# Gated attention with a routed mixture of experts: slot tiles loaded in pairs, positions made one step sooner, zeros on ScalarE's queue, late low parts on GpSimd

## The reference

```python
xn = layernorm(x)
q, k, v = split(xn @ w_qkv.T + b_qkv)
s = (softmax(q @ k.T / sqrt(512)) @ v) @ w_out.T + b_out          # attention, one head of width 512
vals, idx = top_k(xn @ router_w + router_b, 2)                    # 8 experts, 2 per token
h = silu(xn @ expert_w[e] + expert_b[e])                          # for the chosen experts e
y = xn + (sum of h, weighted by softmax(vals)) @ proj_w + proj_b
out = x + s * silu(norm_w * y / rms(y))
```

## Time and profile before

| what | value |
|---|---|
| median of 3 runs | 536.72 us (535.99 to 538.28) |
| profiled execution, its own time | 537.63 us |
| span of its trace | 535.7 us |
| TensorE busy | 499.5 us, 93% |
| VectorE busy | 305.9 us, 57% |
| ScalarE busy | 204.1 us, 38% |
| GpSimd busy | 178.7 us, 33% |

### The profile page before, as it was taken

How to read it: one execution, slowest core, us unless ns; L and a number is a source line. 1 busy time by engine, 2 the same in 40 slices (tenths; PEclk the granted TensorE clock), 3 DMA queues, 4 the chain that set the end, 5 groups by cost and what they waited for, 6 DMA issues and landing times.

```text
span 535.7 us, 7525 instructions
## 1 busy us (share of the span) xinstructions
PE 499.5 (93%) x2234; PEld 411.1 (77%) x2235; DVE 305.9 (57%) x462; ACT 204.1 (38%) x300; POOL 178.7 (33%) x278
## 2 busy tenths in 40 slices
PE   4999999999999949578989999999999999999996
PEld 2688778887898837466767888789888889888884
DVE  2557232764224315499768888875565753667552
ACT  0264542143023133345333444432364553335550
POOL 3053210003888730000000000157457754275144
PEclk9999999999999969879999999999999999999999
DMA  7761269992786777585767555698513632252202
GB/s 268 263 237 39 95 218 400 406 408 103 229 281 237 255 256 215 158 230 165 211 214 218 190 193 179 205 351 297 192 64 118 197 102 76 71 154 91 79 21 98
DMA packets 69836, 104.22 MB, mean 195 GB/s; under 512 B 7200, under 2 KB 31280, under 8 KB 69808
## 3 DMA queue, kind: packets, MB, share of 16 engines
q1 hardware_dynamic: 60576, 75.26, 41.9%
q0 software_dynamic: 7360, 25.19, 13.7%
q10 hardware_dynamic: 1872, 3.41, 2.1%
HBM read 60.32 MB, written 43.52 MB: 194 GB/s over the span
## 4 chain that ended last, share of the span: by engine, by line
PE 55%; SPq 13%; POOL 10%; issue 8%; DMA 6%; DVE 6%; ACT 1%; DVEq 0%; ACTq 0%; POOLq 0%
PE ab L1394 10%; PE ab L1395 10%; PE ab L1396 10%; SPq L459 9%; POOL rows_scratch L652 6%; PE sc L1394 5%; PE sc L1396 5%; PE sc L1395 5%; PE tp L1400 3%; PE sc L1411 3%; POOL W L641 3%; SPq L502 2%; DMA y_scratch<-yt 2%; DVE tp L1175 2%; PE tp L1445 2%
## 5 line engine op out<-in xcount | busy, mean ns | idle before, releaser
L663 POOL DMA_INDIRECT y<-y_scratch,pos x32 | 31.3, 980 | 159.7 <-DMA y_scratch<-yt 144.4
L1394 PE MATMUL ab<-W,st_h 128*128 x156 | 63.9, 410 | 14.8 <-DVE st_l L1122 9.9
L1395 PE MATMUL ab<-W,st_h 128*128 x156 | 62.5, 400 | 0.0
L1396 PE MATMUL ab<-W,st_l 128*128 x156 | 62.4, 400 | 0.0
L652 POOL DMA_INDIRECT rows_scratch<-xb,pos x32 | 31.2, 974 | 63.7 <-DVEq L1118 55.5
L1394 PEld LDWEIGHTS ab<-W,st_h 128*128 128x128 f32 x156 | 30.4, 195 | 26.1 <-issue 20.0
L1394 PE MATMUL sc<-xt_h,t_h 128*128 128x512 f32 x128 | 50.3, 393 | 0.0
L1396 PE MATMUL sc<-xt_h,t_l 128*128 128x512 f32 x128 | 49.9, 390 | 0.0
L1395 PE MATMUL sc<-xt_l,t_h 128*128 128x512 f32 x128 | 49.8, 389 | 0.0
L868 ACT ACTIVATE yt<-yt 128x512 f32<-128x512 f32 x39 | 24.6, 632 | 48.9 <-DVE yt L1252 48.9
L1183 DVE TENSOR_REDUCE small<-sc 128x1 f32<-128x1024 f32 x16 | 19.6, 1224 | 31.8 <-PE sc L1396 31.7
(11 more groups left out here) (257 smaller groups left out, 1230.2 us busy)
## 6 DMA issues: line engine op xcount, KB each, us to landing
rows_scratch<-xn SPq DMA_DIRECT2D x3, 3328.0 KB, 24.4
y_scratch<-yt SPq DMA_DIRECT2D x39, 256.0 KB, 2.2
xb<-in_expert_w POOLq DMA_DIRECT2D x6, 1024.0 KB, 6.1
xn<-rows_scratch SPq DMA_DIRECT2D x96, 64.0 KB, 2.0
xg<-rows_scratch SPq DMA_DIRECT2D x92, 64.0 KB, 2.2
rows_scratch<-xs SPq DMA_DIRECT2D x16, 256.0 KB, 2.0
xb<-rows_scratch SPq DMA_DIRECT2D x16, 256.0 KB, 7.3
x<-in_x SPq DMA_DIRECT2D x16, 256.0 KB, 2.8
```

What stands on the lines that cost most here:

```text
L663: pool.indirect_dma_start(y[:, q, :], None, y_d, bass.IndirectOffsetOnAxis(pos[:, GB * s + p:GB * s + p + 1], 0))\
L1394: nc.tensor.matmul(dst, lh, rh, start=start, stop=False)
L1395: nc.tensor.matmul(dst, lh, rl, start=False, stop=False)
L1396: return nc.tensor.matmul(dst, ll, rh, start=False, stop=stop)
```

## The change

Six edits: (a) the last piece of `choose` runs after `pt_low(1)` and before `attn_out(0)`; `early_high(0)` moves from query tile (0, 2) to (0, 1), GpSimd makes `early_low(2, ...)` in scatter tiles 12 to 15 in place of 8 to 11, and the loads of rows to send are regrouped. (b) The zero DMAs leave by ScalarE's queue, during the values of batch 0. (c) Slot tiles are loaded two at a time, with four DMAs of 128 KB and two semaphores. (d) The first loads are reordered in SP's queue, and the two peeled `w_low` with `turn` and `g_low` in VectorE's. (e) The low parts m = 2 to 9 are GpSimd's (`w_lp`), m = 0 and 1 stay VectorE's (`BY_VEC = 2`). (f) `mw` is written in another order of columns, so that `key_weights` reads whole blocks.

```diff
-        EARLY_AT = ((0, 2), (0, 3), (1, 0), (1, 3))
+        EARLY_AT = ((0, 1), (0, 3), (1, 0), (1, 3))
+        BY_VEC = 2
+        def lows_done(k):
+            m = 2 * (k + 1 - EARLY)
+            return (w_lo, m) if m <= BY_VEC else (w_lp, m - BY_VEC)
@@ SyncE
-            def load_tile(i, q):
+            def load_pair(i, n, tiles=2):
                 for a in range(4):
-                    sp.dma_start(rows[q][32 * a:32 * (a + 1), :].rearrange("p (r f) -> p r f", r=4),
-                                 rows_q[ds(i, 1), a, :, :, :].rearrange("o s r f -> s (o r) f")).then_inc(xg_in[q], 16)
-            def load_next(i, q):
-                sp.wait_ge(g_t, i - 3)
-                load_tile(i, q)
+                    w = slice(32 * a, 32 * (a + 1))
+                    sp.dma_start(pairs[n][w, 0:tiles, :].rearrange("p t (r f) -> p (t r) f", r=4),
+                                 rows_q[ds(i, tiles), a, :, :, :].rearrange("t s r f -> s (t r) f"))\
+                        .then_inc(pair_in[n], 16)
+            def load_next(i, n, tiles=2):
+                sp.wait_ge(g_t, i - 2)
+                load_pair(i, n, tiles)
-            sp.wait_ge(zero_set, 1)
-            for n in range(3):
-                w = slice(n * SLOT_TILES // 3, (n + 1) * SLOT_TILES // 3)
-                sp.dma_start(rows_t[:, w, :], zeros.to_broadcast([P, w.stop - w.start, D])).then_inc(zero_in, 16)
             for j in range(GB):
                 (bias loads at j == QB + 1 as before)
+                if j == QB + 2:
+                    sp.wait_ge(ptr_done, 1 + GB)
+                    load_pair(2, 1)
+                if j == QB + 3:
+                    load_next(6, 1)
                 sp.wait_ge(ab_read, 2 + U["a", 0, j] + 1)
                 sp.dma_start(s_g[j], so[:, j % 2, :]).then_inc(so_st[j % 2], 16)
                 if 1 <= j <= 3:
-                    for g in range(GB + 2 * j - 2, GB + 2 * j if j < 3 else G):
+                    for g in range(GB + 3 * j - 3, min(GB + 3 * j, G)):
                         load_to_send(g)
-                if j == QB + 1:
+                if j == QB:
                     for g in range(GB):
                         sp.wait_ge(sent[g], 64)
-                    for i in range(2):
-                        load_tile(i, i)
+                    load_pair(0, 0)
                 if j == QB + 2:
-                    (loads of tiles 2 and 3, then 4 to 7 behind the loop)
+                    load_next(4, 0)
@@ the looped tiles
-                for q in range(4):
-                    store_y(4 * i + q, q % 2)
-                    load_next(4 * i + q + 8, q)
+                for n in range(2):
+                    store_pair(4 * i + 2 * n)
+                    load_next(4 * i + 2 * n + 8, n)
@@ GpSimd
-                if g < 3 * KC:
+                if g < 2 * KC:
                     early_low(g // KC, g % KC)
+                elif g >= 3 * KC:
+                    early_low(2, g % KC)
             for c in range(KC):
                 early_low(3, c)
+            for m in range(BY_VEC, LATE):
+                _, whole, high, low = halves(m)
+                pool.wait_ge(w_hi, m + 1)
+                pool.tensor_tensor(low, whole, high, ALU.subtract).then_inc(w_lp, 1)
@@ ScalarE
+            def clear_slots(n):
+                w = slice(n * SLOT_TILES // 3, (n + 1) * SLOT_TILES // 3)
+                act.dma_start(rows_t[:, w, :], zeros.to_broadcast([P, w.stop - w.start, D])).then_inc(zero_in, 16)
                 v_hi(0, t)
+                if t >= GB - 3:
+                    act.wait_ge(zero_set, 1)
+                    clear_slots(t - GB + 3)
             def load_next(k):
-                act.wait_ge(w_lo, 2 * (k - 1 - EARLY))
+                act.wait_ge(*lows_done(k - 2))
@@ VectorE
                 pt_low(1)
+                go_on()
                 attn_out(0)
                 row_max(QB * i + 3)
-                go_on()
...
             for i in range(PEEL):
                 add_bias(i, i % 2, i < 2)
                 g_low(i + 2, i % 2)
                 turn(i + 4, i % 4, i // 4 + 1)
-                if i < LATE - AHEAD:
-                    w_low(i + AHEAD)
@@ fold of the keys (n >= KC), high and low parts alike
+                    out, whole = by_fours(out), in_fours(whole)
@@ TensorE, key_weights
-                    last = product(bank(("t", b, i, n)), every_fourth(left[:, 0, c, :], n), every_fourth(left[:, 1, c, :], n),
+                    w = slice(n * P, (n + 1) * P)
+                    last = product(bank(("t", b, i, n)), left[:, 0, c, w], left[:, 1, c, w],
                                    right[0][:, c, q], right[1][:, c, q], c == 0, c == KC - 1)
```

More of the change, by code:

```diff
@@ L216, in gated_attention_moe @@
         rows = (xn[:, 0, :], xn[:, 1, :], xg[:, 0, :], xg[:, 1, :])
+        pairs = (xn, xg)
         mw1_rows = mw1[:, :, :, :].rearrange("p a c n -> p (a c) n").bitcast(F32)
@@ L298, in gated_attention_moe @@
         w_lo = sem("w_lo")
+        w_lp = sem("w_lp")
         be_in = sem("be_in")
-        xg_in = sems("xg_in", 4)
+        pair_in = sems("pair_in", 2)
         g_t = sem("g_t")
@@ L350, in home, with in_fours, by_fours @@
             return SLOT_TILES + (g + GB if g < GB else g - GB)
+        def in_fours(v):
+            return v.rearrange("p (q c) -> p q c", c=KC)
+        def by_fours(v):
+            return v.rearrange("p (c q) -> p q c", c=KC)
         def raw_in(k):
@@ L746, in fold_high @@
                 k = n if n < KC else FOLDS[n - KC]
-                nc.scalar.copy((nw_h if n < KC else mw_h)[:, k, :], sc[:, k // 2, k % 2, :]).then_inc(fold_h, 1)
+                out, whole = (nw_h if n < KC else mw_h)[:, k, :], sc[:, k // 2, k % 2, :]
+                if n >= KC:
+                    out, whole = by_fours(out), in_fours(whole)
+                nc.scalar.copy(out, whole).then_inc(fold_h, 1)
             def normalise(g):
@@ L875, in load_next @@
             def load_next(k):
-                act.wait_ge(w_lo, 2 * (k - 1 - EARLY))
+                act.wait_ge(*lows_done(k - 2))
                 load_raw(act, k)
             act.wait_ge(s_done, GB)
-            for m in range(AHEAD):
-                w_high(m)
-                if m == 1:
-                    load_next(BY_POOL)
-                    g_split(0, 0, True)
-                    g_split(1, 1, True)
+            w_high(0)
+            w_high(1)
+            g_split(0, 0, True)
+            g_split(1, 1, True)
+            load_next(BY_POOL)
+            w_high(2)
+            w_high(3)
             for i in range(PEEL):
@@ L1024, in fold_low @@
                 k = n if n < KC else FOLDS[n - KC]
-                vec.tensor_tensor(l[:, k, :], sc[:, k // 2, k % 2, :], h[:, k, :], ALU.subtract).then_inc(fold_l, 1)
+                low, whole, high = l[:, k, :], sc[:, k // 2, k % 2, :], h[:, k, :]
+                if n >= KC:
+                    low, whole, high = by_fours(low), in_fours(whole), by_fours(high)
+                vec.tensor_tensor(low, whole, high, ALU.subtract).then_inc(fold_l, 1)
             def fold_value_bias():
@@ L1170, in turn @@
             def turn(i, q, j, first=False):
-                dve.wait_ge(xg_in[q], 64 * (j + 1))
+                dve.wait_ge(pair_in[q // 2], 64 * (j + 1))
                 if not first:
@@ L1230, in attention_block @@
                     turn(1, 1, 0, True)
-                    w_low(0)
-                    w_low(1)
-                attn_out(2)
-                if tail:
-                    g_low(0, 0)
-                    turn(2, 2, 0)
-                    g_low(1, 1)
-                    turn(3, 3, 0)
-                    w_low(2)
-                    w_low(3)
+                    for m in range(BY_VEC):
+                        w_low(m)
+                    g_low(0, 0)
+                    g_low(1, 1)
+                    turn(2, 2, 0)
+                    turn(3, 3, 0)
+                attn_out(2)
                 attn_out(3)
@@ L1672, in attend_late @@
                 attend(1, j, high, low, v1_h, v1_l)
-            pe.wait_ge(w_lo, LATE)
+            pe.wait_ge(w_lp, LATE - BY_VEC)
             turn_comb(0)
```

39 lines of the change are left out of this document (19 added, 20 removed).

## The result

The changed kernel takes 512.04 us (median of 4 runs, 506.97 to 512.65) against 537.50 (535.99 to 538.88) for the kernel before beside it: a ratio of 0.951 (95% interval 0.944 to 0.957). On a second chip six runs gave 515.35 (510.05 to 517.67) against 537.51, a ratio of 0.960 (0.958 to 0.963). The profiled execution took 512.65, its span is 510.8. Forecast were 507 for the median and 507.7 for the profiled execution. The time lies in the stated range of 502 to 516, but 1 us above the likeliest branch (502 to 511), and 5.0 us of the forecast gain of 29.9 are missing. Single executions on the second chip reached 517.67, above the range.

What follows compares the result with a forecast made beforehand. TensorE, busy 93%, was taken as the bound, losing 33.2 us between 189.8 and 341.29; 29.7 + 0.7 - 0.5 = 29.9 us off 537.63 gave 507.7 profiled, 507 median, range 502 to 516.

Steps and rivals of the forecast that it cites:

- (a) Positions: Routing and scatter: `routed` 9.3 us sooner, scatter landed at 182.1, gaining 7.2 us of TensorE idle and half clock behind it.
- R4: Rival at the scatter: it comes no sooner, as zeros or a raw set hold GpSimd; 517 us, chance 0.05.
- (b) Zeros: Zero DMAs on ScalarE's queue: third issue held until 57.5 to 59.5, price 0.5 us; otherwise they cost the scatter 4 us.
- R1: Rival in batch 0's values: early zeros hold up ScalarE or the row stores, 2 to 7 us, about 513; chance 0.15.
- (c) The loop: Looped slot tiles: SP's issues per pair take 4.5 us against TensorE's 5.46, so TensorE sets the pace, 2.73 a tile.
- R3: Rival in the looped tiles: they miss 2.73 us, half of the loop's 8 us stays; 511 us, chance 0.10.
- The peel: First slot tiles: bank free and tile 0 at 200.3, stalls of 1.4, 0.8, 1.1 us, tile 7 ends at 226.1.
- R5: Rival: slower, as a pair of slot tiles lands late; gain gone at a landing of 8.6 us; chance 0.02.
- the prediction's three causes: Lost TensorE time: scatter wait 7.23 us, VectorE's 3.55 us peel step against 2.73, SP's load issuing in looped tiles.
- R2: Rival in the peel: its weight chain is longer than stepped, 3 to 6 us and a half-clock spell; 512, chance 0.13.
- (e): Peel: VectorE's step without `w_low` falls from 3.55 to 2.35 us, under TensorE's 2.73.
- (f): `key_weights`: matmuls 0.2276 us apart instead of 0.2347, 192 of them save 1.4 us; strided folds up to as much again.

Runs made afterwards that it cites:

- f_positions_late: attn_first with the last piece of the routing (`choose`) moved back behind `row_max(3)`: 523.66 us, 0.973.
- f_zeros_on_sp: attn_first with the three zero DMAs back on SyncE's queue, behind the first eight `load_to_send`: 518.98 us, 0.964.
- f_single_loads: attn_first with each pair of slot tiles loaded by eight DMAs of 64 KB instead of four of 128 KB: 527.95 us, 0.983.
- attn_first: Changed kernel with VectorE's `attn_out(2)` and `attn_out(3)` put before the turns of tiles 2 and 3: 510.66 us, 0.949.
- store_first: attn_first with the load of tiles 6 and 7 issued behind the last store of the attention output: 509.82 us, 0.947.
- changed_again: The changed kernel unedited, run again on the second chip: 515.35 us, 0.960.
- f_lows_on_vector: attn_first with the low parts m = 2 to 9 back on VectorE: 511.31 us, 0.951.

## Why the prediction came out as it did

**(a) Positions: the times right, the use of them other than forecast.** GpSimd's first and last issue of the scatter, then ScalarE's copy for expert 1 and the exponential behind it:

```profile
119.20 1.08 POOL L669 DMA_INDIRECT rows_scratch<-xb,pos  x1 [44.22 <-DVEq L1156]
...
174.34 0.98 POOL L669 DMA_INDIRECT rows_scratch<-xb,pos  x1 [0.30 <-issue]
```

```profile
183.54 1.91 ACT L863 CAST W<-xb 128x2048 fp32r<-128x2048 f32 x1
185.35 1.11 ACT L883 ACTIVATE prob<-sc,small 128x1024 f32<-128x1024 f32 x1
```

The forecast had the first issue near 119.6, the last at 174.8 and, with TensorE 1.5 us ahead, the copy at 183.9. The copy waits for no DMA. R4 is out. The landing of 7.31 that the step took over was 2.7 us here. By f_positions_late this matters: with the positions late and the other edits in place, a landing of 2.7 and a last issue 2.2 us sooner left 0.8 us of the stall of 7.2. So most of that stall would have gone without the move, and costing the move by it was wrong. What the prediction did not see is the larger use of the lead: a scatter 10 us later costs 12.6 us, through the landings of the pair and of the attention outputs' stores. The two cannot simply be added, since in that run the base was another kernel than the one before.

**(b) Zeros: right, price not paid.** ScalarE's last issue of zeros and its next work:

```profile
52.90 5.20 ACTq L804 DMA_DIRECT2D rows_scratch<-xn  x1
59.06 2.93 ACT L779 ACTIVATE xs<-xb,shift,rstd 128x512 f32<-128x512 f32 x4 [5.58 <-POOL shift L422]
```

The third issue was held until 58.1 (forecast 57.5 to 59.5), the second not at all, and the normalisation starts 0.1 us later than before: the 0.5 us taken is nought. For zeros left on SP the prediction had a cost of 4 us; f_zeros_on_sp measures 8.0, the scatter being about 6 us late and the rest of the price lying in the landings behind it. R1 also said that the row stores starve. The queues from 60 to 66 us (packets, MB, share of the engines; the first is ScalarE's with the zeros, the second SyncE's):

```profile
q10 hardware_dynamic: 947, 1.94, 86.9%
q1 hardware_dynamic: 189, 0.36, 16.3%
```

The row stores took 6.0 us in the median instead of 2.0. ScalarE waited 2.5 us for them, TensorE nowhere more than before: its stretch from 47 to 75 is busy 27.43 of 28. The starved 3.2% of the earlier trace rows did not come back with both queues at work, and neither did equal shares.

The Trainium skill (DMA: Bandwidth & Descriptors, Queues, rings and completion order) lets a DMA engine take turns between queues at packet granularity. SyncE's four stores were all issued or being issued in these 6 us, and the packets (as the profile counts them, of about 2 KB) went 947 to 189; the trace agrees with a share for each, not with equal ones. The prediction's reading of it, about twice the time alone at no cost, came out at three times (2.0 to 6.0) and at no cost to TensorE.

**(c) The loop: right.** 57.00 of 57 us busy, tiles 2.72 us apart; R3 is out. f_single_loads shows that the four larger DMAs carry it: with eight small ones the same stretch is busy 52.52 us.

**The peel: the step that failed.** The prediction said that VectorE's tail, "11.0 us from 190.2", frees the bank at 200.3. The 11.0 us hold work alone (its parts, as listed, add up to 11.3). Taken without the wait of 4.72, the first `attn_out` ends at 204.47 - 4.72 = 199.75: the work was sized well, the term that was missing is the landing of the pair in the middle of it. The only landing that the prediction used for slot tiles was the 2.2 us of the old median, and the risk of a late pair was weighed for the loop alone (R5). With 2.2 us behind the last issue at 191.0 the rows would have lain there at 193.2, before VectorE asked at 196.8; they came at 201.5. In the profiled execution it cost 4.4 us for the idle time and 2.4 for the half clock, less the 0.6 behind: 6.2. That the idle time would bring a half-clock spell was not in the sum either.

The trace of the kernel before had the same thing, and none of the prediction's three causes names it. VectorE's turn of tile 2 waited for its rows with the last `attn_out` behind it, and TensorE stood 4.92 us before slot tile 1 for that bank (VectorE's line, then TensorE's):

```profile
213.04 1.09 DVE L1175 STREAM_TRANSPOSE tp<-xg 128x512 f32<-128x512 f32 x1 [5.30 <-DMA xg<-rows_scratch]
...
219.24 0.61 PE L1394 MATMUL ab<-W,st_h 128*128 x1 [4.92 <-DVE so L1210]
```

Freeing the bank does not bring the forecast back. attn_first gains 5.8 us on its chip, net of the waits that then appear, and at 510.66 it is still 3.7 us above 507. Its tile 0 is 1.1 us sooner than stepped, tile 8 1.5 us later and the first matmul of batch 1's values (312.88) 2.4 us later. So the peel behind tile 0 was stepped too short as well.

**The other steps of the peel.** Tile 3's wait for the attention output's store, stepped to 209.3, is hidden behind the late tile 0 in the changed kernel; with the bank freed it appears at 210.46, and store_first removes it. The stalls for raw weights, stepped at 3.3 us before tiles 5, 6 and 7, did not come in the profiled execution. TensorE has three waits of 1.8 us in all, before tiles 4, 6 and 7, but behind each stands VectorE's bias, which had waited 1.16, 1.05 and 1.70 us for a result's store to land (in 4.3, 4.4 and 6.2 us). The last of them:

```profile
227.31 0.69 DVE L1287 TENSOR_TENSOR yt<-ab,bias_e 128x512 f32<-128x512 f32 x1 [1.70 <-DMA y_scratch<-yt]
```

Only changed_again has a wait for weights, 0.9 us before tile 6. The first two raw sets landed in 10.1 and 7.9 us (6.1 stepped), the last two, on which the price of R2 stood, in 5.4 and 6.7. R2's number, 512, is the one measured, and its mechanism is not: that the two meet is chance.

**(e)** was thought to bring VectorE's step from 3.55 to 2.35 us and with it the pace of the peel. f_lows_on_vector shows the step as forecast, 3.54 us with the low parts back on VectorE, and denies its price: the time is the same within the intervals. Without the low parts the peel isn't at TensorE's pace either. It waits for landings and stores, and in attn_first eight matmuls at half clock take back a part of what the shorter step gives.

**(f)** 1.6 us by itself (1.0 to 2.2 by the interval), 1.4 forecast: right. The strided fold costs more than a plain one, ScalarE's copies (ns min/median/max) of the two kinds in the changed kernel:

```profile
L773 ACT CAST nw<-sc x4: 585/585/586, 20.8 to 23.4; 128x512 fp32r<-128x512 f32 x4
L773 ACT CAST mw<-sc x4: 1067/1076/1116, 61.9 to 73.0; 128x512 fp32r<-128x512 f32 x4
```

That is the upper bound of the forecast, "as much again", nearly reached, and beside `fold_keys` it cost nothing: TensorE's wait for ScalarE in this part is 0.6 us, as in the trace before.

**The undone edits do not add up.** From attn_first, 27 us under the kernel before, they take 12.6, 8.0, 18 and 0, and (f) 1.6 by another route: 40 us, and (d) isn't among them. The traces show where they meet: undoing (a), (b) or (c) each ends in the same wait, VectorE's bias of tile 1 for the store of the attention output that stands behind a pair load in SP's order. TensorE stands 5.2, 5.8 and 6.0 us for it before tile 3, and 1.8 in attn_first. store_first takes that store out of the way; no run undoes an edit on top of it, so what each is worth there is open.

**What stays open**: why the slowest of the four equal loads needs about 5 us longer than the median of them (8.9 to 10.5 against 4.8 to 5.6 in four traces). Its variation may be the spread of the changed kernel, 507 to 518 us, since attn_first, where the bank does not hang on it, spreads less; only two profiled executions of the unedited kernel (a wait of 3.4 us at 510.05, of 4.9 at 512.65) stand for it, and no run tests it. Nor does a run say why the changed kernel is at 0.951 on one chip and at 0.960 on another.

## What to carry to other kernels

Take a transfer's landing from the traffic that will lie beside it at that moment, not from the median over the trace: here it was 2.2 us by the median and 10.5 where it decided. In a hand-written order, put the short work that frees a bank or a buffer before any instruction that waits for a DMA; the same holds for a store behind loads in an issuing queue, which held TensorE for 5 to 6 us in three of the runs. When edits lean on the same resource, undo them one at a time from the best version, expect the prices to exceed the gain, and read in each trace which wait pays.

## What the runs showed of the hardware

- Four equal DMAs of 128 KB issued within 2 us of each other, with the DMA engines busy, landed between 3.9 and 10.5 us; the slowest of the four took 8.9, 10.0, 10.1 and 10.5 us in four profiled executions with the same loads near it.
- The same store of 256 KB (`s_scratch<-so`) landed in 3.4 us in the changed kernel and in 7.9 in f_positions_late.
- TensorE ran about 12 matmuls at 1.2 GHz after 4.88 us of idle time and 13 after 3.40 us in changed_again (granted clock 0.50 from 203.00 to 208.71), eight (from 211.96, 0.43 us apart) soon after 1.83 us of it in attn_first, and none in that stretch of store_first after 3.51 us (granted clock 1.00 from 212 to 232). The length of a single gap does not decide.
- Writing 128x512 with 128 elements from one to the next cost ScalarE 1076 ns instead of 585 and VectorE, which also reads the high part so, 1100 instead of 681 (medians).
- A weight load of 128x128 took TensorE 312 ns in steps of four elements and 188 out of whole blocks.
- GpSimd needed 2.34 to 2.40 us for a 128x1024 low part, twice VectorE's 1.20.
- Of three DMAs of 3.3 MB on ScalarE's queue the third held the engine for 5.2 us, the second for 0.4; on SP in the kernel before the second was held as well.
